# An FFN kernel's last group of output rows: summed on the chip and stored plainly, instead of accumulated in memory

## The reference

```
x = x + L0_ffn(L0_cond(x))                 # phase A: a projection with LoRA and bias
x = x + L1_ffn(L1_cond(x))                 # phase B
L1_cond: per batch element a rank-16 adapter, out = (x @ B_sel.T) @ A_sel.T
L1_ffn:  W = NF4[codes] * scales           # gate, up: 2752 x 1024, down: 1024 x 2752, blocks of 64
         inter = silu(x @ Wg.T) * (x @ Wu.T)
         out   = inter @ Wd.T
```

## Time and profile before

| what | us |
|---|---|
| median of 3 runs (1100.24 to 1100.74) | 1100.68 |
| the profiled execution's own time | 1100.7 |
| its span, from the first to the last instruction | 1099.0 |
| TensorE busy | 1026.5 (93% of the span) |
| VectorE busy | 813.6 (74%) |
| ScalarE busy | 806.4 (73%) |
| GpSimd busy | 213.1 (19%) |

### The profile page before, as it was taken

One profiled execution on the slowest core, in us unless ns is written; L12 is line 12 of the kernel. 1 busy time (PEld: TensorE's weight loads), 2 busy tenths in 40 slices (PEclk: granted clock), 3 DMA queues, 4 the chain that ended last, 5 costly groups with the idle time before them and its releaser, 6 DMA issues.

```text
span 1099.0 us, 14511 instructions
## 1 busy us (share of the span) xinstructions
PE 1026.5 (93%) x5352; PEld 861.5 (78%) x5352; DVE 813.6 (74%) x815; ACT 806.4 (73%) x961; POOL 213.1 (19%) x285
## 2 busy tenths in 40 slices
PE   4899999999999889899999999999989999899995
PEld 3588888988888767778778778787878877788884
DVE  4778887878787788778888888888887788871220
ACT  4767777776677788878888888888888888863341
POOL 4003223232221111111111111121111211122111
PEclk9899999999999998999999999999999999999998
DMA  9735444464342366565645446455554645534667
GB/s 245 220 96 137 102 124 116 109 154 110 85 98 58 58 115 111 100 115 96 115 82 92 96 96 115 97 95 96 102 100 87 116 80 103 106 58 68 107 114 115
DMA packets 62950, 117.89 MB, mean 107 GB/s; under 512 B 6272, under 2 KB 38544, under 8 KB 62880
## 3 DMA queue, kind: packets, MB, share of 16 engines
q0 software_dynamic: 17504, 59.80, 34.7%
q1 hardware_dynamic: 44048, 56.11, 17.7%
q10 hardware_dynamic: 1328, 1.05, 0.3%
HBM read 58.22 MB, written 67.11 MB: 114 GB/s over the span
## 4 chain that ended last, share of the span: by engine, by line
PE 54%; DVE 24%; ACT 10%; issue 9%; SPq 2%; DMA 1%; DVEq 0%; POOL 0%; ACTq 0%
DVE val L692 12%; PE ps_z L1009 12%; PE ps_y L1009 11%; PE ps_z L886 10%; PE ps_gu L991 6%; DVE val L694 5%; ACT ring L525 5%; PE ps_t L928 3%; PE ps_t L920 3%; PE ps_gu L928 3%; ACT inter L629 2%; PE ps_y L875 2%; PE ps_gu L903 2%; DVE val L711 1%; DVE wd_late_lo L736 1%
## 5 line engine op out<-in xcount | busy, mean ns | idle before, releaser
L525 ACT ACTIVATE ring<-codes 128x1024 f32<-128x1024 int32 x455 | 455.4, 1053 | 119.2 <-DVE val L692 114.5
L692 DVE TENSOR_TENSOR val<-val,ring 128x1024 f32<-128x1024 f32 x260 | 318.1, 1223 | 15.2 <-issue 0.2
L694 DVE SCALAR_TENSOR_TENSOR val<-ring,val 128x1024 f32<-128x1024 f32 x195 | 238.0, 1220 | 11.1 <-ACT ring L525 2.5
L819 DVE TENSOR_TENSOR inter<-ps_gu,inter 128x512 f32<-128x512 f32 x88 | 60.7, 690 | 149.6 <-ACT inter L629 149.6
L497 POOL DMA_DIRECT2D out<-staged x96 | 82.6, 860 | 379.0 <-ACT staged L643 375.1
L886 PE MATMUL ps_z<-we_hi,y_hi 128*128 128x512 f32 x256 | 105.5, 412 | 3.6 <-DVE y_lo L744 3.6
L886 PE MATMUL ps_z<-we_hi,y_lo 128*128 128x512 f32 x256 | 101.1, 395 | 0.0
L886 PE MATMUL ps_z<-we_lo,y_hi 128*128 128x512 f32 x256 | 100.9, 394 | 0.0
L629 ACT ACTIVATE inter<-ps_gu 128x512 f32<-128x512 f32 x88 | 51.7, 587 | 62.9 <-PE ps_gu L991 62.3
L920 PE MATMUL ps_t<-ident,val 128*128 128x128 f32 x520 | 70.9, 280 | 20.0 <-DVE val L711 19.1
L1009 PE MATMUL ps_y<-wd_late_hi,in_hi 128*128 128x512 f32 x256 | 82.1, 402 | 6.9 <-DVE in_lo L825 5.5
(11 more groups left out here) (117 smaller groups left out, 1829.8 us busy)
## 6 DMA issues: line engine op xcount, KB each, us to landing
out<-staged POOLq DMA_DIRECT2D x96, 512.0 KB, 5.3
codes<-in_L_ffn_gate_codes SPq DMA_DIRECT2D x21, 512.0 KB, 3.5
codes<-in_L_ffn_up_codes SPq DMA_DIRECT2D x21, 512.0 KB, 3.7
codes<-in_L_ffn_down_codes SPq DMA_DIRECT2D x21, 512.0 KB, 4.0
xs<-in_x SPq DMA_DIRECT2D x16, 512.0 KB, 3.6
out<-in_L_ffn_bias SPq DMA_DIRECT2D x4, 2048.0 KB, 13.2
out<-xs POOLq DMA_DIRECT2D x16, 512.0 KB, 5.5
w_stage<-in_L_ffn_W SPq DMA_DIRECT2D x8, 512.0 KB, 9.9
```

The lines of the kernel that those rows point to most:

```text
L525: act.activation(ring[:, (k - 1) % RING, :], codes[:, n % 2, :], ACT.Identity, bias=offset, scale=slope).then_inc(lines, 1)
L692: ins = dve.tensor_tensor(v, v, line, pick)
L694: ins = dve.scalar_tensor_tensor(out=v, in0=line, scalar=add, in1=v, op0=ALU.add, op1=pick)
L819: dve.tensor_tensor(inter[:, q % 2, :], ps_u[:, :], inter[:, q % 2, :], ALU.mult).then_inc(inter_ready, 1)
```

## The change

In the last group (slots from LAST = 80 on) the partial sum no longer goes to memory through ScalarE and an accumulating transfer of GpSimd.

- SyncE reads the rows back (`read_back`) into the five places of `ring`, which the decoding has left by then, four tiles ahead; for each it waits until the accumulation of the tile's slot in group 4 has landed, and from the sixth tile on until the place's earlier store has.
- VectorE adds PSUM and the rows read back, in place (`sum_out_rows`, 128 x 1,024), behind the `product` and `inter_lo` of its slot.
- SyncE stores the sum plainly (`store_sum`).
- `down` waits for that sum (`out_sum`) from slot 82 on, where it waited for ScalarE's copy.
- The last tile (slot 95) is made half by half: eight matmuls for the first 512 columns, then eight for the others; each half is summed and stored by itself.
- ScalarE's `evac_out` and GpSimd's `accumulate` end with slot 79; GpSimd's last waits are for that, and SyncE waits for all stores at its end.

```diff
+    LAST = NT * (NG - 1)
...
+            def read_back(t):
+                place, before = t % RING, LAST + t - NT
+                if t == 0:
+                    sp.wait_ge(combo, COMBOS * NU)
+                if t >= RING:
+                    sp.wait_ge(sum_out[place], 16 * (t // RING))
+                sp.wait_ge(acc_out[before % OS], 16 * (before // OS + 1))
+                sp.dma_start(ring[:, place, :], out_rows[t * P:(t + 1) * P, :]).then_inc(back_in[place], 16)
+
+            def store_sum(t):
+                if t == NT - 1:
+                    for h in range(2):
+                        sp.wait_ge(out_sum, t + h + 1)
+                        sp.dma_start(out_rows[t * P:(t + 1) * P, h * HALF:(h + 1) * HALF],
+                                     ring[:, t % RING, h * HALF:(h + 1) * HALF]).then_inc(sum_out[t % RING], 16)
+                else:
+                    sp.wait_ge(out_sum, t + 1)
+                    sp.dma_start(out_rows[t * P:(t + 1) * P, :], ring[:, t % RING, :]).then_inc(sum_out[t % RING], 16)
+
+            for t in range(RING - 1):
+                read_back(t)
+            for t in range(NT):
+                store_sum(t)
+                if t + RING - 1 < NT:
+                    read_back(t + RING - 1)
+            for place in range(RING):
+                tiles = range(place, NT, RING)
+                sp.wait_ge(sum_out[place], 16 * (len(tiles) + (NT - 1 in tiles)))
...
-            for slot in range(NT * NG):
+            for slot in range(LAST + 1):
...
-            accumulate(NT * NG - 1)
             for place in range(OS):
-                pool.wait_ge(acc_out[place], 16 * len(range(place, NT * NG, OS)))
+                pool.wait_ge(acc_out[place], 16 * len(range(place, LAST, OS)))
...
-                    if slot:
+                    if 0 < slot <= LAST:
                         evac_out(slot - 1)
...
-            evac_out(NT * NG - 1)
...
+            def sum_out_rows(t, h=None):
+                cols = slice(0, D) if h is None else slice(h * HALF, (h + 1) * HALF)
+                dve.wait_ge(down_mm, LAST + t + 1 + (h or 0))
+                dve.wait_ge(back_in[t % RING], 16 * (t // RING + 1))
+                dve.tensor_tensor(ring[:, t % RING, cols], ps_o[t % 2][:, cols], ring[:, t % RING, cols], ALU.add
+                                  ).then_inc(out_sum, 1)
...
                         low_wd(before)
+                    if slot > LAST:
+                        sum_out_rows(slot - 1 - LAST)
...
+            sum_out_rows(NT - 1, 0)
+            sum_out_rows(NT - 1, 1)
...
-            def down(g, t, ks):
+            def down(g, t, ks, halves=(0, 1)):
...
-                if slot >= 2:
+                if slot >= LAST + 2:
+                    pe.wait_ge(out_evac, LAST)
+                    pe.wait_ge(out_sum, slot - 1 - LAST)
+                elif slot >= 2:
                     pe.wait_ge(out_evac, slot - 1)
...
-                        for h in range(2):
+                        for h in halves:
...
+                    if slot == NT * NG - 1:
+
+                        for h in range(2):
+                            down(g, t, range(chunks), (h,))
+                        continue
```

More of the change, by code:

```diff
@@ L233, in adaln_ffn @@
         acc_out = [sem(f"acc_out{k}") for k in range(OS)]
+        back_in = [sem(f"back_in{k}") for k in range(RING)]
+        sum_out = [sem(f"sum_out{k}") for k in range(RING)]
         consts_ready = sem("consts_ready")
@@ L281, in adaln_ffn @@
         out_evac = sem("out_evac")
+        out_sum = sem("out_sum")
         def wait(eng, semaphore, count):
```

## The result

| | us |
|---|---|
| changed kernel, median of 4 runs (1088.87 to 1091.13) | 1089.95 |
| kernel before, median of 4 runs (1100.24 to 1100.80) | 1100.71 |
| ratio, 95% interval | 0.9904 (0.9888 to 0.9920) |
| forecast, range | 1093.4, 1091.8 to 1098.5 |
| the profiled execution after: time, span | 1088.87, 1087.2 |

The profiled execution is the fastest of the four.

A forecast was written before the change was run, and what follows sets the result against it. TensorE was taken to bound the last group without a break, followed by a 13.35 us tail, nearly half GpSimd's DRAIN. 1099.0 − 9.1 (tail) + 1.75 (gaps) = 1091.65, plus 1.7 around the span: 1093.4 forecast, range 1091.8 to 1098.5.

The forecast's parts named there:

- the Sum's first term: Whole kernel: the starting figure 1099.0 us, the profiled execution's span before the change.
- 1099.0 − 9.1 + 1.75 = 1091.65: Whole span: old span, less the tail's saving, plus TensorE's new waits; 1.7 around the span made it 1093.35.
- the store's and the waits' bounds: Main case's ends: 1091.8 with store 2.1 and waits 0.9, 1096.7 with store 5.5 and waits 2.4.
- The tail: Behind TensorE's last matmul: 4.24 us instead of 13.35, 9.1 less, with GpSimd's DRAIN hidden under the remaining matmuls.
- The store: Kernel's end: SyncE's plain 256 KB store of the last half lands 2.9 us after its issue.
- the lower bound: Last store: from below, GpSimd's 16 KB loads, which land after 2.1 us.
- SyncE's DRAIN: Kernel's end: taken at 0.2 us, between 0.37 right behind an issue and at best nothing.
- The gaps: Last group: TensorE waits for VectorE's sum at slots 84, 88 and 92, 0.58 us each, 1.75 in all.
- Hidden edits: Read-backs, reordered last tile and TensorE's second wait cost no time; the wait 0.7 us if not hidden.
- The first: Rival at the kernel's end: the DRAIN closes behind the program's last transfer, so 1099.2, no change; chance 0.11.
- The second: Rival in the last group: each new gap drops TensorE's granted clock, 1.7 us three times, 1098.5; chance 0.08.
- The third: Rival at the kernel's end: the plain store lands as late as the worst load, 15.6 us, time 1106; chance 0.03.

The follow-up runs named there:

- Experiment 5: Changed kernel with VectorE's sum put ahead of `inter_lo` of the same slot: 1089.33 us, 0.9903 of the kernel before.
- experiment 3: Changed kernel, but GpSimd waits for the last store before it ends: 1097.06 us, 0.9982 of the kernel before.
- experiments 2 and 8: The changed kernel run again unchanged, beside the kernel before: 0.9932 of before (7.5 us less) in the former, 1092.03 us (0.9924) in the latter.
- experiments 8 and 9: Run beside each other: the changed kernel unchanged, 1092.03 us (0.9924 of before), and the changed kernel with VectorE's sum ahead of `inter_lo`, 1089.40 us (0.9898).

## Why the prediction was right or wrong

*What failed is the Sum's first term.* "1099.0 − 9.1 + 1.75 = 1091.65" takes the head of one profiled execution for that of every execution, and adds that "the median of the runs (1100.68) is the same within 0.02". The runs shown agreed with it only because they all lay in the upper part of a wider spread: over 23 further runs the same kernel took 1096.65 to 1101.47. The changed kernel's first four runs lay at the lower end of its own: 1089.95 less 1.7 around the span and 75.3 for group and tail leaves a head of 1012.9, against 1015.4, so 2.5 us of the 10.8 lie in work that the change doesn't touch. In the two profiled executions most of that difference is TensorE's granted clock; for the medians this is argued from the clocks beside the times. With the other terms as measured below, 1093.4 − 2.5 − 1.1 + 0.2 = 1090.0, which is the time. In two further comparisons with more runs the change was worth 7.5 and 7.8 us. The range failed with the head: its lower end was made of the store's and the waits' bounds, and had nothing for it.

*The tail: right in mechanism, 1.1 us too long.* The DRAIN went under the matmuls, at 1018.9 where I had some 1022 less the head's 3.5. The store was mis-sized: 2.9 taken, 2.0 measured. That is just below the lower bound, a load of 16 KB from GpSimd's queue (2.1), which was no bound for a store from SyncE's. Of SyncE's loads of 256 KB the prediction weighed two (5.1 to 5.5) and overlooked the two of the down codes, which landed after 3.4. And SyncE's DRAIN took 0.007 and not 0.2. The rest (release, half sum of 0.69, signals) came out as forecast: 3.14 against 4.24. The Trainium skill's formula ("DMA: Bandwidth & Descriptors", "Anatomy of one DMA": some 2.0 us fixed, the rest by size) gave an estimate of 2.6 for the half store, nearer than my own term but above the 2.0 measured; for 512 KB its estimate is 3.2, and the rows show 2.6 at the least and 2.9 in the median. That section is on transfers issued by GpSimd, and these stores are SyncE's, which the prediction didn't say. That the fixed part is the larger one, the trace does bear out: half the bytes saved 0.6 of 2.6 us, so that by an estimate from these two stores 1.4 are fixed.

*The gaps: right.* Three, at slots 84, 88 and 92, as forecast; 0.36 + 0.28 = 0.64 us each against 0.58, 1.92 in all against 1.75. Experiment 5 shows their cause.

*Hidden edits: right.* Read-backs, reordered last tile and the second wait cost TensorE nothing: in experiment 5, which has them all, the last group takes 70.28 us, as before. The read-backs were slower than the 3.6 us assumed, 4.6 in the median and 9.6 at the most; being issued four slots ahead covered that.

*The rivals.* The first, that the DRAIN stays last, is refuted by the closing rows; experiment 3 gets it back at the end only by making GpSimd end last. The section of the Trainium skill named there ("Runtime: NRT & Kernel Launch", "The ~15µs preamble/postamble breakdown") gives its total as depending on the number of engines and the setup of the DMA, not as the same whatever the kernel does; no run here varied those. The second, a fall of the clock behind the new gaps, did not come: the granted clock was 1.00 from 1010 to 1084 us, and the tiles after each gap run at 3.63 us again from the second one on. The third, a late store, did not come either: 2.0 us.

So the change itself is worth 10.2 − 1.9 = 8.3 us where 7.35 were forecast. With the head of the profile before, that gives 1092.4, inside the range.

*What stays open.* Why the granted clock falls in one execution and not in the next at the same instructions, and whether the first comparison's two ends met by chance or by how each program was loaded; no experiment separated the two. What GpSimd's DRAIN waits for is open too.

## What to carry to other kernels

Before costing an edit, look at what each engine's sequencer does behind its last instruction: here an engine's DRAIN of 6 us was nearly half of the tail, and letting that engine finish early removed it. When a consumer moves to another engine, price its place in that engine's queue; here putting the sum ahead of `inter_lo`, which TensorE needed only later, took the last group back by the 1.9 us, and that version's medians (1089.33 and 1089.40) are below those of the changed kernel in experiments 2 and 8. And put the spread of the work that an edit doesn't touch into the range: a few runs that agree are no bound for it.

## What was not expected of the hardware

- One kernel's executions differ by 5 us (1096.65 to 1101.47) with a mean granted clock from 0.988 to 0.984, on one core with identical instructions, and medians over 11 and 23 runs of it by 1.5 us. Beside experiments 8 and 9 its 11 runs spread over 6.9 us (1095.86 to 1102.80, clock 0.989 to 0.982).
- GpSimd's DRAIN took 5.75 to 6.07 us in every kernel whose GpSimd had waited for its transfers, even 70 us after the last of them, and 10.1 us when it began with one under way.
- A plain store of 512 KB landed after 2.9 us in the median (2.6 at the least, 6.0 at the most), sooner than the load of that size in the earlier trace rows (3.6) and in about half the time of an accumulating store (5.5).
